# A two-layer graph network on one core: the second gather of the first layer becomes an accumulating one

## The chip, the cores and the metric

One core of a Trainium2 chip. The metric is device time in microseconds of one launch; lower is better. Before the change the median of 3 runs is 4833.23 us (4825.9 to 4849.17).

## The reference, cut to what matters

3125 nodes with 160 features (64 scalars and 32 vectors of three components), 100000 edges sorted by destination. Layer 0 is an attention layer over the edges, layer 1 a convolution with a segment sum. Of layer 0 the part that the change touches is the message of an edge, the sum of a row of its source node and a row of its destination node:

```python
s_n, v_n = _equiv_layernorm(s, v, gamma_s, beta_s, gamma_v)
src, dst = (edge_index[0], edge_index[1])
msg_s = (s_n @ Ws_src)[src] + (s_n @ Ws_dst)[dst]
msg_v = jnp.einsum('ncx,cd->ndx', v_n, Wv_src)[src] + jnp.einsum('ncx,cd->ndx', v_n, Wv_dst)[dst]
y0, y1 = (rsh[:, 0], rsh[:, 1:4])
w1 = rbf @ W_rbf
m1_s, m1_v = _cg_tp(msg_s, msg_v, y0, y1, w1[:, :CS], ...)
...
agg = jax.ops.segment_sum(alpha * h, dst, num_segments=n)
```

`_cg_tp` multiplies the message with the edge's weights and its direction; two more stages of small matrix products and such products follow, then a softmax over the edges of each destination and the segment sum.

## The kernel before

The kernel runs in stages, each of which all engines go through together.

- **Nodes.** 25 tiles of 128 nodes are normalised and multiplied with the weights. The rows for sources and destinations (160 floats, 640 bytes each) are written to two tables in HBM, `src_tab` and `dst_tab`.
- **Layer 0, first sweep.** The edges are worked off in 392 rounds of 256: 128 partitions, two edges on each (`G = 2`). This is the long stage, and the one that the change is in.
- **Layer 0, softmax and segment sum** (`stage_c`): maxima by scans, exponentials, then 49 windows whose sums GpSimd adds to `sum_tab` with accumulating transfers to HBM (line 698).
- **Layer 1.** Again 392 rounds, with one gathered table (`hid_tab`, line 721, two indirect transfers in a round), and 49 accumulating transfers to `agg_tab` (line 698). Then the output.

Each engine has its own program, written out by hand, and waits for the others at semaphores. `loop_steps` runs a function `stage(t)` for t = 0, 1, 2, ...; every part of it is called with an offset, so `gather0(t + 3)` works three rounds ahead of t. A step object `v` names the buffers of a round: `slot8` is round modulo 8, `par` modulo 2, `sslot` the half of the index buffer (four rounds share one load of indices; they are a group, whose first round has `place` 0).

In a round of the first sweep:

- **SP** (`sp0`) loads the indices of a group (`load_places`, line 487) when the group two before it has all its gathers landed (semaphores `LA["ga"]`), loads the inputs of the weights (`load_rbf`, line 496), and stores the result of the round two before (`store`, line 507, to `h_tab`).
- **GpSimd (POOL)** (`pool0`, `gather0`, line 658) issues four indirect transfers of 128 rows each: two from `src_tab` into `gat0`, two from `dst_tab` into `gatd`. Before them it waits until VectorE has used up the buffers (`LA["m"]`), and at the first round of a group for the indices (`LA["ix"]`). In the profile's rows `gat0` is called ACC and `gatd` SC, for the large tiles that hold them; each has 8 buffers. The transfers of a round raise `LA["ga"][slot8]` by 64.
- **VectorE (DVE)** (`stage0`) adds the two rows of the round (`messages`, line 1478, behind the wait for `LA["ga"]`), makes the products of round t+1 (`products0` and what follows, lines 1503 to 1529, the last of which raises `LA["m"]`), and between these works on round t-1 (lines 1540 to 1593) and t-2 (lines 1603 and 1612). Line 1503 waits for the sum of line 1478.
- **TensorE (PE)** transposes the products (line 800) and multiplies them with weights (lines 792, 822, 824, 847, 849); **ScalarE (ACT)** copies, weighs and applies the sigmoid.

The order in `stage0` before:

```python
gated(t + -1, total)
added = messages(t + 1, total)
ups = gated_up(t + -1, total)
done = summed(t + -1, total, ups)
parts = products0(t + 1, total, added)
scaled(t + -1, total, done)
```

## Time and profile before

| what | value |
|---|---|
| median of 3 runs | 4833.23 us |
| lowest, highest | 4825.9, 4849.17 us |
| span of the profiled execution, first to last instruction | 3828.1 us |
| what lies around the span, by the median | 1005.1 us |
| busy in the span: PE, PEld, DVE, ACT, POOL | 89%, 69%, 92%, 81%, 67% |
| first sweep of layer 0 in the span | about 86 to 2218 us |
| softmax and segment sum of layer 0, nodes between the layers | about 2218 to 2656 us |
| rounds of layer 1 | about 2656 to 3772 us |
| mean granted TensorE clock | 0.974 of full speed |

The profiled execution has no time of its own in the list beside its span; the 1005.1 us are the median less that span, and hold what runs before the first and after the last instruction of the program.

How to read it: the busy share of an engine is the share of the span in which it executed something that isn't a branch, a semaphore or the issue of a DMA. The idle time before a group of instructions is given with what ended it: "<-issue" is time in which the engine waited for nothing that the profile shows. An indirect transfer on POOL counts as busy while its descriptors are made, not while its bytes move; in what follows "a transfer on POOL" is that time. VectorE's instructions overlap a little in the rows, so a short wait between two of them may not show as idle time.

### The profile page before, as it was taken

How to read it: one execution, taken by the hardware profiler on the slowest of the kernel's cores; microseconds unless marked ns; L12 is line 12 of the kernel's file. 1: busy time of each engine (PE TensorE's matmuls, PEld its weight loads, DVE VectorE, ACT ScalarE, POOL GpSimd, SP SyncE). 2: the span in 40 equal slices, each digit the busy share in tenths (PEclk: the TensorE clock that was granted, in tenths of full speed). 3: DMA queues.
4: the chain of work that ended last, by engine and by line, in shares of the span. 5: the costliest groups of instructions: out<-in, count | busy, mean ns of one | idle time of the engine just before them, and what ended most of it. 6: DMA issues, size and time to landing. Idle time of an engine off the chain costs nothing. (4 is left out here: it accounts for less than half of the span.)

```text
span 3828.1 us, 96308 instructions
## 1 busy us (share of the span) xinstructions
PE 3407.1 (89%) x21340; PEld 2641.0 (69%) x21340; DVE 3541.0 (92%) x12738; ACT 3089.1 (81%) x11217; POOL 2570.9 (67%) x2469
## 2 busy tenths in 40 slices
PE   4899999999999999999999939976999999999997
PEld 3888888888888888888888838864333333333335
DVE  5999999999999999999999978874999999999995
ACT  4888899899989988988899847754787877778774
POOL 1777777777777777777777711111777777777772
PEclk8999999999999999999999979987999999999999
DMA  4333333333333333333333359971333433343333
GB/s 110 89 95 92 92 95 94 92 95 93 95 94 93 95 92 94 93 93 93 94 93 95 93 186 270 274 204 44 92 94 95 95 94 95 95 95 93 95 94 115
DMA packets 299642, 411.02 MB, mean 107 GB/s; under 512 B 98580, under 2 KB 234772, under 8 KB 299316
## 3 DMA queue, kind: packets, MB, share of 16 engines
q0 software_dynamic: 127008, 208.99, 24.2%
q1 hardware_dynamic: 172564, 201.26, 16.3%
q8 instruction: 24, 0.39, 0.0%
q14 instruction: 46, 0.38, 0.0%
HBM read 309.09 MB, written 100.94 MB: 107 GB/s over the span
## 5 line engine op out<-in xcount | busy, mean ns | idle before, releaser
L658 POOL DMA_INDIRECT SC<-dst_tab,idx x784 | 904.5, 1154 | 238.8 <-issue 237.3
L721 POOL DMA_INDIRECT ACC<-hid_tab,idx x784 | 811.4, 1035 | 348.6 <-issue 340.3
L658 POOL DMA_INDIRECT ACC<-src_tab,idx x784 | 758.5, 967 | 313.1 <-issue 164.2
L800 PE MATMUL TR<-ident,M 128*128 128x128 f32 x4704 | 664.4, 277 | 136.9 <-DVE M L1529 135.5
L800 PEld LDWEIGHTS TR<-ident,M 128*128 128x128 f32 x4704 | 520.1, 141 | 229.9 <-DVE M L1529 229.8
L1124 ACT ACTIVATE MT<-TR 128x768 f32<-128x768 f32 x784 | 596.9, 825 | 3.5 <-PE TR L800 3.5
L1113 ACT ACTIVATE ACC<-W,ACC 128x64 f32<-128x64 f32 x2352 | 577.7, 336 | 0.0
L849 PE MATMUL HP<-w_hv,MT 128*128 128x128 f32 x3136 | 520.2, 288 | 0.0
L824 PE MATMUL E<-w_mv,MT 128*128 128x128 f32 x3136 | 476.7, 275 | 0.0
L824 PEld LDWEIGHTS E<-w_mv,MT 128*128 128x128 f32 x3136 | 436.6, 191 | 0.0
L1306 ACT ACTIVATE ACC<-TR,y 128x128 f32<-128x128 f32 (+1 forms) x1568 | 417.2, 551 | 1.3 <-PE TR L982 1.2
L849 PEld LDWEIGHTS HP<-w_hv,MT 128*128 128x128 f32 x3136 | 413.2, 192 | 0.0
L1306 ACT ACTIVATE TAB<-TR,y 128x128 f32<-128x128 f32 (+1 forms) x1568 | 412.7, 422 | 0.0
L997 PE MATMUL HP<-M,ohE 128*128 128x480 f32 x800 | 374.4, 591 | 20.2 <-DVE M L1853 18.9
L792 PE MATMUL W<-w_rbf,rbf 128*128 128x224 f32 x1568 | 364.2, 355 | 15.9 <-DMA rbf<-in_rbf_line 13.7
L997 PE MATMUL E<-M,ohE 128*128 128x480 f32 x768 | 358.7, 590 | 17.5 <-DVE M L1853 16.1
L822 PE MATMUL E<-w_ms,MT 128*128 128x168 f32 x1568 | 355.0, 308 | 7.4 <-issue 4.7
L982 PEld LDWEIGHTS TR<-w_edge,ACC 64*128 64x128 f32 x1568 | 119.4, 186 | 322.5 <-ACT TAB L1306 157.5
L982 PE MATMUL TR<-w_edge,ACC 64*128 64x224 f32 x1568 | 255.9, 403 | 32.7 <-ACT TAB L1306 30.3
L1111 ACT ACTIVATE ACC<-W,ACC 128x96 f32<-128x96 f32 x784 | 272.4, 347 | 11.5 <-issue 11.5
L792 PEld LDWEIGHTS W<-w_rbf,rbf 128*128 128x128 f32 x1568 | 268.1, 192 | 16.8 <-issue 13.8
L847 PE MATMUL HP<-w_hs,MT 128*128 128x64 f32 x1568 | 265.7, 251 | 3.0 <-ACT MT L1124 3.0
(278 smaller groups left out, 7662.5 us busy)
## 6 DMA issues: line engine op xcount, KB each, us to landing
h_tab<-ACC SPq DMA_DIRECT2D x392, 160.0 KB
SC<-h_tab SPq DMA_DIRECT2D x50, 640.0 KB, 4.8
TAB<-h_tab SPq DMA_DIRECT2D x48, 640.0 KB, 5.2
ACC<-in_e64T SPq DMA_DIRECT2D x98, 256.0 KB
ACC<-src_tab,idx POOLq DMA_INDIRECT x784
SC<-dst_tab,idx POOLq DMA_INDIRECT x784
ACC<-hid_tab,idx POOLq DMA_INDIRECT x784, 3.4
agg_tab<-ACC POOLq DMA_DIRECT2D x49, 240.0 KB, 4.0
```

The costliest lines, as they stand in the source:

```text
L658: pool.indirect_dma_start(gat[:, v.slot8, g, :], None, table.ap(), bass.IndirectOffsetOnAxis(ap=idx[:, v.sslot, c + g:c + g + 1], axis=0))\
L721: pool.indirect_dma_start(gat1[:, v.slot8, g, :], None, hid_tab.ap(), bass.IndirectOffsetOnAxis(ap=idx[:, v.sslot, c:c + 1], axis=0))\
L792: ins = nc.tensor.matmul(W1[:, 224 * g:224 * (g + 1)], rbf[:, v.sslot, v.place, g, :], w_rbf[:, :], start=True, stop=True)
L800: ins = nc.tensor.transpose(to[:, b * G + g, :], Mt[:, g, lo:lo + w], ident[:, :])
L822: nc.tensor.matmul(E1[:, 0, ES * g:ES * (g + 1)], MT[:, 0, g, :], w_ms0[:, :], start=True, stop=True)
L824: ins = nc.tensor.matmul(E1[:, 1, P * g:P * (g + 1)], MT[:, 1 + b, g, :], w_mv0[:, b, :], start=(b == 0), stop=(b == 1))
L849: ins = nc.tensor.matmul(HP[:, P + P * g:P + P * (g + 1)], MT2[:, 1 + b, g, :], w_hv0[:, b, :], start=(b == 0), stop=(b == 1))
L982: ins = nc.tensor.matmul(Wr[v.par][:, g, 0:224], hid[hg, v.qslot, P * v.quad_place:P * (v.quad_place + 1)], w_edge1[hg, :], start=True, st ...
L997: ins = nc.tensor.matmul(AG[v.sslot][:, 0:MW], ohE[:, v.slot, g, :], M[:, v.par, g, :], start=(v.place == 0 and g == 0), stop=(v.place == ...
L1113: ins = nc.scalar.activation(o[:, 160 + 64 * k:224 + 64 * k], w[:, 160:224], ACT.Copy, scale=y_at(v, g, 1 + k))
L1124: nc.scalar.activation(dst[:, 0:3].rearrange("p k g e -> p (k g e)"), tr[:, 0:3 * G, :].rearrange("p a e -> p (a e)"), ACT.Copy).then_inc( ...
L1306: ins = nc.scalar.activation(WS[v.slot][:, g, P * k:P * k + hi - lo], wg_[:, lo:hi], ACT.Copy, scale=y1[:, v.sslot, c:c + 1])
```

## The change

The rows of the destination are no longer fetched into a buffer of their own and added by VectorE. They are fetched by an indirect transfer that adds them to the rows of the source, which are already in `gat0`. Such a transfer may only be issued when the plain gather below it has landed, so the gather of the source rows is asked for six rounds ahead instead of three, and the adding transfer three rounds ahead. SP's load of the indices moves from seven rounds ahead to eight. `gatd` and `messages` are gone; the wait for the landed rows stands at the head of `products0`.

```diff
-        gatd = scf[:, 0:8 * G * D].rearrange("p (b g f) -> p b g f", b=8, g=G)
...
             def sp0(t, total):
-                load_places(t + 7, total)
+                load_places(t + 8, total)
                 load_rbf(t + 5, total)
                 store(t + -2, total)
-            loop_steps(sp, Q, NS, False, 7, 2, sp0)
+            loop_steps(sp, Q, NS, False, 8, 2, sp0)
...
+            def gather_src(v, total):
+                if not inside(v, total):
+                    return
+                if v.past(7):
+
+                    wait(LA["m"], v.num - 6)
                 if v.place == 0:
                     wait(LA["ix"][v.sslot], v.sup_round(16))
...
+                for g in range(G):
+                    c = 2 * v.place + g
+                    pool.indirect_dma_start(gat0[:, v.slot8, g, :], None, src_tab.ap(),
+                                            bass.IndirectOffsetOnAxis(ap=idx[:, v.sslot, c:c + 1], axis=0))\
+                        .then_inc(LA["ga"][v.slot8], 16)
+
+            def add_dst(v, total):
+
+                if not inside(v, total):
+                    return
+                wait(LA["ga"][v.slot8], v.slot_round(64, 8) - 32)
+                for g in range(G):
+                    c = 2 * Q + 2 * v.place + g
+                    pool.indirect_dma_start(gat0[:, v.slot8, g, :], None, dst_tab.ap(),
+                                            bass.IndirectOffsetOnAxis(ap=idx[:, v.sslot, c:c + 1], axis=0),
+                                            compute_op=ALU.add)\
+                        .then_inc(LA["ga"][v.slot8], 16)
 
             def pool0(t, total):
-                gather0(t + 3, total)
-            loop_steps(pool, Q, NS, False, 3, 0, pool0)
+                gather_src(t + 6, total)
+                add_dst(t + 3, total)
+            loop_steps(pool, Q, NS, False, 6, 0, pool0)
...
-            def messages(v, total):
-
-                if not inside(v, total):
-                    return
-                dve.wait_ge(LA["ga"][v.slot8], v.slot_round(64, 8))
-                row = gat0[:, v.slot8, :, :]
-                return ch.count(TT(row, row, gatd[:, v.slot8, :, :], ALU.add))
...
+            def products0(v, total):
+
+                if not inside(v, total):
+                    return None
                 dve.wait_ge(LA["ga"][v.slot8], v.slot_round(64, 8))
...
-                added = messages(t + 1, total)
                 ups = gated_up(t + -1, total)
                 done = summed(t + -1, total, ups)
-                parts = products0(t + 1, total, added)
+                parts = products0(t + 1, total)
```

The queue of POOL in the middle of the first sweep, with what each row waits for (a_m is `LA["m"]`, a_ix0 the landing of a group's indices). Before, two rounds read:

```order
L658 DMA ACC<-src_tab,idx 128x160 [waits a_m]
L658 DMA ACC<-src_tab,idx 128x160
L658 DMA SC<-dst_tab,idx 128x160 x2
L644 REGISTER_ALU
L644 REGISTER_ALU [waits a_m]
L658 DMA ACC<-src_tab,idx 128x160 [waits a_ix0]
L658 DMA ACC<-src_tab,idx 128x160
L658 DMA SC<-dst_tab,idx 128x160 x2
```

and now (a_ga4 and a_ga5 are the landings in two of the eight buffers):

```order
L657 DMA ACC<-src_tab,idx 128x160 [waits a_m]
L657 DMA ACC<-src_tab,idx 128x160
L668 DMA ACC<-dst_tab,idx 128x160 [waits a_ga4]
L668 DMA ACC<-dst_tab,idx 128x160
L643 REGISTER_ALU
L643 ISA [waits a_m]
L657 DMA ACC<-src_tab,idx 128x160 [waits a_ix0]
L657 DMA ACC<-src_tab,idx 128x160
L668 DMA ACC<-dst_tab,idx 128x160 [waits a_ga5]
L668 DMA ACC<-dst_tab,idx 128x160
```

There are four transfers in a round as before; the last two now write the same tile as the first two, of an earlier round, and wait for its landing.

At the very start of the stage POOL's queue now reads:

```order
L657 DMA ACC<-src_tab,idx 128x160 [waits s_tab0d,a_ix0]
L657 DMA ACC<-src_tab,idx 128x160 x7
L668 DMA ACC<-dst_tab,idx 128x160 [waits a_ga0]
L668 DMA ACC<-dst_tab,idx 128x160
L657 DMA ACC<-src_tab,idx 128x160 [waits a_ix1]
```

Eight plain gathers stand ahead of the first adding pair, where two stood ahead of the first pair from `dst_tab`.

## Rows read from the trace of the kernel before

**Rows 1.** Busy time by stage: first sweep, rounds of layer 1.

```profile
core 0: us, PE busy (x) PEld busy (x) DVE busy (x) ACT busy (x) POOL busy (x), PEclk, DMA share, GB/s
102.00:2218.00 2116.00, 1979.12 (x15485) 1855.71 (x15484) 2096.20 (x8519) 1906.76 (x6968) 1643.54 (x1551) 1.00 0.35 93
2656.00:3772.00 1116.00, 1037.45 (x3332) 422.85 (x3332) 1039.24 (x3527) 869.41 (x3284) 860.43 (x833) 0.99 0.39 93
```

**Rows 2.** Groups on POOL, 102 to 2218 us: busy, mean ns, idle before.

```profile
L658 POOL DMA_INDIRECT SC<-dst_tab,idx x775 | 894.3, 1154 | 236.1 <-issue 234.6 <-DVE M L1529 1.5
L658 POOL DMA_INDIRECT ACC<-src_tab,idx x776 | 750.7, 967 | 236.7 <-issue 162.1 <-DVE M L1529 74.6
```

**Rows 3.** Timeline of the start of the sweep, POOL's gathers and VectorE's addition.

```profile
84.02 0.95 POOL L658 DMA_INDIRECT SC<-dst_tab,idx  x1 [0.30 <-issue]
85.27 0.94 POOL L658 DMA_INDIRECT ACC<-src_tab,idx  x1 [0.30 <-issue]
...
86.55 0.49 DVE L1478 TENSOR_TENSOR ACC<-ACC,SC 128x320 f32<-128x320 f32 x1 [17.83 <-DMA SC<-dst_tab,idx]
...
91.57 0.49 DVE L1478 TENSOR_TENSOR ACC<-ACC,SC 128x320 f32<-128x320 f32 x1 [2.47 <-DMA SC<-dst_tab,idx]
...
96.54 0.49 DVE L1478 TENSOR_TENSOR ACC<-ACC,SC 128x320 f32<-128x320 f32 x1 [1.88 <-DMA SC<-dst_tab,idx]
```

**Rows 4.** Timeline in mid-sweep: POOL's transfers and VectorE beside them.

```profile
1006.25 0.95 POOL L658 DMA_INDIRECT SC<-dst_tab,idx  x1 [0.30 <-issue]
...
1007.50 1.55 POOL L658 DMA_INDIRECT SC<-dst_tab,idx  x1 [0.30 <-issue]
...
1010.68 0.49 DVE L1478 TENSOR_TENSOR ACC<-ACC,SC 128x320 f32<-128x320 f32 x1
...
1011.09 0.35 DVE L1546 TENSOR_TENSOR svy<-E,ACC 128x192 f32<-128x192 f32 x1
...
1023.42 1.81 POOL L658 DMA_INDIRECT SC<-dst_tab,idx  x1 [0.30 <-issue]
```

**Rows 5.** VectorE's addition, 102 to 2218 us: group, and its waits.

```profile
L1478 DVE TENSOR_TENSOR ACC<-ACC,SC 128x320 f32<-128x320 f32 x388 | 190.4, 491 | 20.3 <-DMA SC<-dst_tab,idx 18.3
```

**Rows 6.** Groups on POOL in layer 1, 2656 to 3772 us.

```profile
L721 POOL DMA_INDIRECT ACC<-hid_tab,idx x784 | 811.4, 1035 | 348.6 <-issue 340.3 <-DVE M L1853 7.7 <-ACT ACC L1317 0.6
L698 POOL DMA_DIRECT2D agg_tab<-ACC x49 | 50.1, 1022 | 9.5 <-issue 9.4
```

**Rows 7.** First transfer of layer 1: the idle time before it.

```profile
2656.38 1.09 POOL L721 DMA_INDIRECT ACC<-hid_tab,idx  x1 [102.84 <-issue]
```

**Rows 8.** The accumulating transfers' line 698: ns min/median/max.

```profile
L698 POOL DMA_DIRECT2D sum_tab<-ACC x49: 841/848/986, 2303.6 to 2552.7; - x49
L698 POOL DMA_DIRECT2D agg_tab<-ACC x49: 984/1023/1055, 2699.9 to 3771.9; - x49
```

**Rows 9.** DMA issues: KB each, median us from issue to landing.

```profile
ACC<-hid_tab,idx POOLq DMA_INDIRECT x784, 3.4
agg_tab<-ACC POOLq DMA_DIRECT2D x49, 240.0 KB, 4.0
...
sum_tab<-ACC POOLq DMA_DIRECT2D x49, 82.0 KB, 5.2
...
gam_v<-in_gamma_v SPq DMA_DIRECT2D x3, 0.1 KB, 1.9
```

**Rows 10.** SP's timeline around a load of indices.

```profile
1021.19 0.35 SPq L487 DMA_DIRECT2D idx<-in_idx_line  x1
1021.79 0.34 SPq L507 DMA_DIRECT2D h_tab<-ACC  x1
```

More of the change, by code:

```diff
@@ L646, in _ @@
             pool.wait_ge(s_tab0d, 160)
-            def gather0(v, total):
+            def gather_src(v, total):
                 if not inside(v, total):
                     return
-                if v.past(4):
-                    wait(LA["m"], v.num - 3)
+                if v.past(7):
+                    wait(LA["m"], v.num - 6)
                 if v.place == 0:
                     wait(LA["ix"][v.sslot], v.sup_round(16))
-                for c, gat, table in ((2 * v.place, gat0, src_tab), (2 * Q + 2 * v.place, gatd, dst_tab)):
-                    for g in range(G):
-                        pool.indirect_dma_start(gat[:, v.slot8, g, :], None, table.ap(),
-                                                bass.IndirectOffsetOnAxis(ap=idx[:, v.sslot, c + g:c + g + 1], axis=0))\
-                            .then_inc(LA["ga"][v.slot8], 16)
+                for g in range(G):
[13 more added lines that the diff above has]
+                        .then_inc(LA["ga"][v.slot8], 16)
             def pool0(t, total):
-                gather0(t + 3, total)
-            loop_steps(pool, Q, NS, False, 3, 0, pool0)
+                gather_src(t + 6, total)
+                add_dst(t + 3, total)
+            loop_steps(pool, Q, NS, False, 6, 0, pool0)
             pool.wait_ge(s_flag, 1)
@@ L1470, in y_of @@
                 return ax(y_all[:, bass.ds(v.column(0), 1), k:k + 1], (4, G), *dims)
-            def messages(v, total):
-                if not inside(v, total):
-                    return
-                dve.wait_ge(LA["ga"][v.slot8], v.slot_round(64, 8))
-                row = gat0[:, v.slot8, :, :]
-                return ch.count(TT(row, row, gatd[:, v.slot8, :, :], ALU.add))
-            def products0(v, total, added):
+            def products0(v, total):
                 if not inside(v, total):
                     return None
-                ch.wait(added)
+                dve.wait_ge(LA["ga"][v.slot8], v.slot_round(64, 8))
                 dve.wait_ge(LA["ws"], v.num + 1)
```

## The prediction

> **What bounds the kernel now.** I read the stages first, then the groups of one engine in the stage that changes, then its timeline, and last the rows of other transfers that price the new one.
>
> By stages, VectorE looks like the bound of the first sweep: it is busy 2096.20 of 2116.00 us, POOL only 1643.54 [rows 1]. That is the share that misleads here. The groups on POOL show an idle time of 0.30 us before every one of its 1551 transfers, never much more, and nearly all of it "issue": it is what POOL needs between two transfers. Busy and idle time together are 894.3 + 750.7 + 236.1 + 236.7 = 2117.8 us [rows 2], the whole of the 2116 us. So **POOL is occupied without a break**, exactly like VectorE. 1551 transfers are 387.75 rounds, one in 5.46 us.
>
> Which of the two leads? At the start of the sweep VectorE waits 2.47 and 1.88 us for the gathered rows, and its additions start 5.02 and 4.97 us apart [rows 3]: POOL's pace with undisturbed transfers, 4 x (0.95 + 0.30) = 5.00 us. POOL never gets a lead. In mid-sweep single transfers are stretched from 0.95 to 1.55 and 1.81 us with the same 0.30 us before them, which no transfer is while VectorE waits [rows 3, 4]. The mean stretch brings the round from 5.00 to 5.46 us. A gather that ends at 1007.50 + 1.55 = 1009.05 is followed by its addition at 1010.68, 1.63 us later; at the start it was 86.55 - (84.02 + 0.95) = 1.58 us, with VectorE idle and waiting [rows 3]. The addition thus begins about when the rows land. The profile books only 18.3 us of waiting there over 388 rounds [rows 5], but with overlapping records short waits don't show. VectorE's own work is 2096.20 / 387.75 = 5.41 us a round, POOL's 5.46 us: two bounds side by side, POOL's the tighter by a hair.
>
> Layer 1 confirms the reading of POOL: 811.4 + 348.6 + 50.1 + 9.5 us, less the 102.84 us before the first transfer, are 1116.8 us in a stretch of 1116 [rows 6, 7]. There too it never rests, and a transfer takes 1.035 us on the mean, 0.09 above the undisturbed one.
>
> **The change, part by part.** The time of reference is the profiled execution's span, 3828.1 us, and the 1005.1 us around it, which is the median 4833.23 by construction; nothing around the span changes.
>
> *VectorE's addition goes.* From its start to the next instruction are 1011.09 - 1010.68 = 0.41 us [rows 4]; VectorE's work falls from 5.41 to 5.00 us a round. Were VectorE the only bound, that would be 0.41 x 392 = 161 us. It is covered by POOL, which still issues four transfers a round and needs 5.46 us for them, so I count it as 0. The wait for the rows moves behind lines 1546, 1554 and 1557, and only line 1503 and what follows now queue behind it; harmless, because the round is set elsewhere.
>
> *Two of four gathers become adding ones.* POOL's time for the plain ones is 2 x (0.967 + 0.305) = 2.54 us, for the pair from `dst_tab` 2 x (1.154 + 0.305) = 2.92 us, 5.46 together [rows 2]. No row shows an indirect transfer that adds. The nearest are the direct accumulating ones of line 698: 0.85 us into `sum_tab` against 0.95 for a plain gather, and in layer 1 1.02 against 1.035 [rows 6, 8]. By them the price is between -0.10 and 0 us more than a gather. From above: an adding row is read, read again at its destination and written, three runs where a copy has two; half as much again is 0.95 x 0.5 = +0.48 us. I take +0.10 us, near the rows of line 698 but on the dear side, because they need no indices and this one needs both. Two a round: 0.20 x 392 = **+78 us** (bounds -78 and +376).
>
> *The stretches.* I keep them as they are, 0.46 us a round. If all went, the round would be 5.00 us, -180 us; if they grew by as much, +180 us. They come with VectorE's instructions, of which one goes, but the rest will run closer together.
>
> The Trainium skill (SBUF — State Buffer, "Who interferes with whom") says that a VectorE instruction with two inputs in SBUF contends with a GpSimd instruction that reads SBUF. The removed addition is one of 16 such instructions in a round and some tenth of their time, so by that page a tenth of the stretches would go with it, 0.05 us a round, 18 us in all, and the sum below would be 4920 us. Rows 3 and 4 agree that only a working VectorE stretches the transfers; which of its instructions does, they don't say.
>
> *The new wait of POOL for the landing of the source rows.* Between that gather and its adding transfer stand 12 others, some 16 us, and rows land 1.6 us after the gather's end [rows 4]. Cost 0. If landing took over 16 us it would stop the queue.
>
> *The loads of indices.* POOL now asks for a group's indices at the gather six rounds ahead, while SP may overwrite that half only when the adding transfers of the group two before have landed. In POOL's queue between the last of those and the first gather that needs the new indices stands one round: 5.46 + 0.30 us. In it must pass the landing of the adding transfer, SP's reaction, and the small load. Before, three more rounds stood there. An accumulating transfer lands 4.0 us after its issue in layer 1 and 5.2 in the segment sum [rows 9], that is 3.0 to 4.4 us after POOL's end of it; the load lands about 1.9 us after its issue (a small load) [rows 9], and I allow 0.3 us for SP. So 5.2 to 6.6 us against 5.8: between 0 and 0.8 us lost in four rounds. I take 0.2, which is 0.05 x 392 = **+20 us** (bounds 0 and +80). Behind SP's wait now stand its stores, one round later than before; 0.6 us after the load they follow [rows 10], and `hst` has four buffers, so no one waits. That cover ends at two rounds of delay.
>
> *Start and end.* The first products need 8 gathers and 2 adding transfers instead of 4 gathers: 6 x 1.25 = 7.5 us later. At the end the last three rounds have only adding transfers and run at VectorE's 5.0 us; about even. **+7 us.**
>
> The transfers themselves: all DMA engines are busy 0.35 of the sweep [rows 1]. The adding ones move more, but even twice the present share stays below the whole. Cost 0. `gatd` leaves SC free, with no effect on others.
>
> **Sum:** 4833 + 78 + 20 + 7 = **4938 us**, a round of about 5.7 us. A measurement of this kernel can tell about 0.5% (24 us) from no change.
>
> **The rivals.**
>
> *Faster: VectorE was the bound.* If POOL's stretches are only what lets it keep step with VectorE (both need 5.4 us, and a transfer never runs into the next round), a shorter VectorE round shortens them, and if adding costs like copying the round falls to 5.0 to 5.1 us: 4833 - 161 + 7 = 4679 us, or 4720 with half of the stretch left. For it: the 2096.20 us of busy time, 99%, and that POOL's and VectorE's periods agree so well. Against it: layer 1's POOL, stretched as well with a busy VectorE, and the additions that start as rows land. Chance 0.18.
>
> The Trainium skill (Perfetto Trace Analysis, "Identifying the Most-Contended Engine") says to optimise first the engine of highest occupancy, which by the busy shares is VectorE; that rule stands behind this rival. The rows on POOL, busy and issue time together, speak against its reading here.
>
> *No change.* Adding costs what copying costs, indices arrive in time, stretches stay: 4833 + 7 = 4840 us. For it: line 698. Chance 0.20.
>
> *Much slower: indices or landings set the round.* The adding transfer lands as late as in the segment sum or later. Then POOL's queue runs dry once in four rounds, 0.8 us or more: 4833 + 78 + 80 + 7 = 4998 us; with an adding transfer at +0.25 us, 5115 us. It decides from a landing of 3.6 us after POOL's end. For it: rows 9. Against it: the segment sum's landing was taken with the DMA engines nearly full. Chance 0.20.
>
> The change does what it says: the order of POOL's queue shows it.
>
> **How the numbers follow.** Forecast 0.42 (4938 us; its own range 4880 to 5040), the rivals 0.18, 0.20 and 0.20. The range must take in most of the slow rival and half of the fast one: 4720 to 5130 us. Faster by over 0.5%, below 4809 us: 0.18 and a little of "no change" by fewer stretches, 0.24. Within 0.5%: 0.16. Slower: 0.60.
>
> **What would show it.** In the new profile of the sweep: VectorE's busy time near 5.0 of 5.7 us a round, with waits at line 1503 for the DMA; POOL's busy and issue time still the whole sweep; line 668 near 1.25 us, line 657 near 0.97; at one in four rounds a gap before line 657 of 0 to 0.8 us. The prediction is wrong if line 668's mean is at or below 1.05 us and the round below 5.4, or if POOL shows gaps that wait for VectorE's line 1529.

## The result, and the profile after

The changed kernel takes **4493.55 us** (median of 4 runs, 4476.52 to 4500.86), the kernel before beside it 4841.2 us (4 runs, 4825.9 to 4868.19): a ratio of **0.9274, 95% interval 0.924 to 0.9308**. Forecast was 4938 us in 4720 to 5130: the change is 7% faster, outside the range and on the other side.

One thing has to be said before any line is read: **the execution whose rows stand ahead of the prediction was not one of those that were timed**, nor like them. It spans 3828.1 us. In the runs below each profiled execution has a time of its own. The kernel before, profiled again, took 4862.71 us and spans 4861.1: 1.6 us lie around the span, not 1005. The same goes for the changed kernel, 4500.86 us and a span of 4499.2. The experiments ran on six chips; on five the kernel before took 4783 to 4846 us, on the sixth 3818.76 us (median of 11), like the first profile. All executions on one chip are of one kind, so this text speaks of the chips; whether it is the chip itself or something that went with it, no run tells. Nearly all that follows is about what those five do and the first profile does not. e1 to e4 shared a chip, so did e5 to e8, e9 to e11, e12 to e14 and e15 to e17, and e18 ran on the sixth; between chips ratios are compared, not times.

By stages, the changed kernel (first sweep, rounds of layer 1), columns as in [rows 1]:

```profile
95.00:2661.00 2566.00, 2081.12 (x15576) 1932.78 (x15576) 1976.51 (x8188) 1948.60 (x7014) 2086.58 (x1557) 0.97 0.40 77
3100.00:4420.00 1320.00, 1110.12 (x3284) 448.66 (x3284) 1028.53 (x3464) 868.53 (x3240) 864.34 (x819) 0.91 0.33 78
```

and the kernel before, profiled again (e1_before), the same stages:

```profile
95.00:3010.00 2915.00, 2249.62 (x15527) 2111.54 (x15526) 2099.47 (x8547) 1946.70 (x6992) 1722.97 (x1557) 0.89 0.25 68
3459.00:4790.00 1331.00, 1114.25 (x3298) 448.82 (x3298) 1036.48 (x3492) 868.11 (x3252) 871.86 (x822) 0.91 0.32 77
```

The sweep is 349 us shorter, layer 1 the same: the gain lies where the edit is. A round (four transfers of GpSimd) takes 2566 / (1557 / 4) = 6.59 us now, 2915 / (1557 / 4) = 7.49 us in e1_before, and took 5.46 us in the first profile. In e1_before no engine is busy for more than 77% of the sweep, and VectorE is idle for 28% of it, where in [rows 1] VectorE never rested and GpSimd was occupied throughout. TensorE's clock is granted at 0.89 of full on the mean; between its two levels, 1.2 and 2.4 GHz, that is the lower one for 22% of the time. In the changed kernel the mean is 0.97.

GpSimd's groups in the sweep (name, busy us, mean ns, idle time before and what ended it), the changed kernel:

```profile
L668 POOL DMA_INDIRECT ACC<-dst_tab,idx x782 | 1305.5, 1669 | 238.3 <-issue 238.3
L657 POOL DMA_INDIRECT ACC<-src_tab,idx x775 | 781.1, 1008 | 236.1 <-issue 215.0 <-DVE M L1533 21.0
```

e1_before:

```profile
L658 POOL DMA_INDIRECT ACC<-src_tab,idx x778 | 976.4, 1255 | 939.1 <-DVE M L1529 699.9 <-issue 239.1
L658 POOL DMA_INDIRECT SC<-dst_tab,idx x779 | 747.4, 959 | 237.7 <-issue 236.8 <-DVE M L1529 0.9
```

In the changed kernel these four numbers fill the sweep: 1305.5 + 781.1 + 238.3 + 236.1 = 2561 of 2566 us. **GpSimd is occupied without a break**, as [rows 2] had it. In e1_before it waits 699.9 us for VectorE's last product. So nothing is gained by less work: the adding transfer costs 1.669 us where the plain one beside it costs 1.008. GpSimd works more and the kernel is faster.

Who was late? VectorE's line 1603 (1607 now) uses TensorE's last product of a round. Its group in the middle of the sweep, in the first profile (500 to 2100 us) and in e1_before (500 to 2500):

```profile
L1603 DVE TENSOR_TENSOR tG<-HP,ACC 128x192 f32<-128x192 f32 x293 | 103.0, 352 | 0.0
```

```profile
L1603 DVE TENSOR_TENSOR tG<-HP,ACC 128x192 f32<-128x192 f32 x268 | 95.4, 356 | 528.9 <-remote 365.7 <-PE HP L849 155.1 <-issue 8.1
```

No idle time before it in the first profile, against 528.9 us in 268 rounds of e1_before, most of it "remote": a signal that the profile ties to no instruction's end. The same group in the changed kernel (500 to 2500):

```profile
L1607 DVE TENSOR_TENSOR tG<-HP,ACC 128x192 f32<-128x192 f32 x304 | 107.8, 355 | 188.1 <-PE HP L861 101.2 <-remote 84.9
```

It still waits, in 195 of 304 rounds, but for 2.1 us at the longest; in e1_before the longest of these waits is 6.2 us. The timeline of e1_before shows one such case (start, length, engine, line, idle time before it):

```profile
1020.34 0.66 PE L849 MATMUL HP<-w_hv,MT 128*128 128x128 f32 x4
...
1022.30 0.82 PE L800 MATMUL TR<-ident,M 128*128 128x128 f32 x6
...
1025.70 0.36 DVE L1603 TENSOR_TENSOR tG<-HP,ACC 128x192 f32<-128x192 f32 x1 [4.33 <-remote]
...
1027.38 0.35 DVE L1529 TENSOR_TENSOR M<-ACC 128x192 f32<-128x192 f32 x1
...
1027.79 1.54 PE L800 MATMUL TR<-ident,M 128*128 128x128 f32 x6 [4.66 <-DVE M L1529]
...
1028.68 0.94 POOL L658 DMA_INDIRECT ACC<-src_tab,idx  x1 [4.25 <-DVE M L1529]
```

The product that line 1603 waits for ends at 1021.00, by the profile; line 1603 starts 4.70 us later. VectorE stands, its products (line 1529) come late, TensorE stands for 4.66 us and then runs its transposes in 1.54 us instead of 0.82, at half the clock, and GpSimd stands for 4.25 us. Call this **a late signal of TensorE**. (These traces lack some of the semaphores' records, so "remote" by itself proves little; the 4.70 us between the product's end and the start of line 1603 don't depend on it. The end of a matmul is modelled by the profiler, so the product itself may have been late.)

### The profile page after: what moved, and what is told of

Its sections match the earlier page's. It is cut to its first block and busy times, and to the rows that moved or that the text cites. A ratio compares the mean times of both kernels' runs of the same rounds, so it can differ in the third digit from the quotient of the medians.

```text
span 4499.2 us, 96352 instructions
## 1 busy us (share of the span) xinstructions
PE 3588.3 (80%) x21340; PEld 2740.0 (61%) x21340; DVE 3413.8 (76%) x12346; ACT 3129.9 (70%) x11217; POOL 3025.2 (67%) x2469
## 2 busy tenths in 40 slices
DMA packets 374905, 411.01 MB, mean 91 GB/s; under 512 B 98580, under 2 KB 322580, under 8 KB 374580
## 5 line engine op out<-in xcount | busy, mean ns | idle before, releaser
L668 POOL DMA_INDIRECT ACC<-dst_tab,idx x784 | 1308.6, 1669 | 238.9 <-issue 238.9
L733 POOL DMA_INDIRECT ACC<-hid_tab,idx x784 | 830.4, 1059 | 554.7 <-issue 352.8
L657 POOL DMA_INDIRECT ACC<-src_tab,idx x784 | 790.0, 1008 | 312.7 <-issue 217.5
L861 PE MATMUL HP<-w_hv,MT 128*128 128x128 f32 x3136 | 536.5, 295 | 0.0
L1009 PE MATMUL HP<-M,ohE 128*128 128x480 f32 x800 | 408.0, 636 | 43.2 <-DVE M L1856 29.9
L1009 PE MATMUL E<-M,ohE 128*128 128x480 f32 x768 | 396.0, 642 | 48.0 <-issue 24.4
L1507 DVE TENSOR_TENSOR M<-ACC 128x192 f32<-128x192 f32 x392 | 140.2, 358 | 376.2 <-DMA ACC<-dst_tab,idx 369.2
L1174 ACT ACTIVATE ACC<-HP 128x128 f32<-128x128 f32 x392 | 109.1, 278 | 447.1 <-DVE ACC L1616 383.9
L804 PE MATMUL W<-w_rbf,rbf 128*128 128x224 f32 x1568 | 388.4, 373 | 15.7 <-DMA rbf<-in_rbf_line 13.6
L1164 ACT ACTIVATE M<-V,ACC 128x96 f32<-128x96 f32 x784 | 252.2, 373 | 115.3 <-DVE V L1571 66.8
```

Source lines behind the costliest of these rows:

```text
L657: pool.indirect_dma_start(gat0[:, v.slot8, g, :], None, src_tab.ap(), bass.IndirectOffsetOnAxis(ap=idx[:, v.sslot, c:c + 1], axis=0))\
L668: pool.indirect_dma_start(gat0[:, v.slot8, g, :], None, dst_tab.ap(), bass.IndirectOffsetOnAxis(ap=idx[:, v.sslot, c:c + 1], axis=0), comp ...
L733: pool.indirect_dma_start(gat1[:, v.slot8, g, :], None, hid_tab.ap(), bass.IndirectOffsetOnAxis(ap=idx[:, v.sslot, c:c + 1], axis=0))\
L804: ins = nc.tensor.matmul(W1[:, 224 * g:224 * (g + 1)], rbf[:, v.sslot, v.place, g, :], w_rbf[:, :], start=True, stop=True)
L861: ins = nc.tensor.matmul(HP[:, P + P * g:P + P * (g + 1)], MT2[:, 1 + b, g, :], w_hv0[:, b, :], start=(b == 0), stop=(b == 1))
L1009: ins = nc.tensor.matmul(AG[v.sslot][:, 0:MW], ohE[:, v.slot, g, :], M[:, v.par, g, :], start=(v.place == 0 and g == 0), stop=(v.place == ...
```

## The experiments

Rounds and clock in the table are read from one view of each kernel, busy time between 500 and 2500 us: 2000 us by a fourth (with a memset a fifth) of GpSimd's instructions, and the mean granted clock. The ratio is to the kernel before on the same chip, with its interval.

| run | edit | round, us | clock | median, us | ratio |
|---|---|---|---|---|---|
| e1_before | none | 7.46 | 0.89 | 4854.16 | 1.001 (0.9988 to 1.0032) |
| e2_no_add | VectorE's addition left out | 7.77 | 0.91 | 4948.13 | 1.0166 (1.0091 to 1.0241) |
| e3_plain | the change, transfers not adding | 7.82 | 0.90 | 4975.75 | 1.0247 (1.0198 to 1.0296) |
| e4_after | the change | 6.56 | 0.98 | 4502.07 | 0.9292 (0.9254 to 0.933) |
| e5_plain_pad | e3 + memset of 1280 | 6.79 | 0.97 | 4587.23 | 0.9589 (0.956 to 0.9619) |
| e6_before_pad | before + memset of 1280 | 6.83 | 0.96 | 4567.19 | 0.9536 (0.9501 to 0.957) |
| e7_plain_pad_half | e3 + memset of 640 | 7.32 | 0.94 | 4778.72 | 0.9975 (0.9946 to 1.0003) |
| e8_after_pad1 | change + memset of 192 in layer 1 | 6.43 | 1.00 | 4453.26 | 0.932 (0.9291 to 0.9349) |
| e9_before_pe | before + 6 transposes | 7.64 | 0.92 | 4907.62 | 1.0162 (1.0106 to 1.0218) |
| e10_after_pe | change + 6 transposes | 6.55 | 0.99 | 4501.45 | 0.9322 (0.9274 to 0.937) |
| e11_after_pad | change + memset of 640 | 7.47 | 1.00 | 4846.53 | 1.0042 (0.9995 to 1.009) |
| e12_before_dve | before + VectorE's 960 | 6.86 | 0.98 | 4613.37 | 0.9534 (0.9496 to 0.9572) |
| e13_before_pe12 | before + 12 transposes | 7.73 | 0.94 | 5010.67 | 1.0342 (1.0299 to 1.0384) |
| e14_half | half of the change | 7.04 | 0.89 | 4702.56 | 0.9731 (0.969 to 0.9772) |
| e15_half_u16 | e14, 16 rounds in a pass | 7.08 | 0.91 | 4726.47 | 0.9759 (0.9715 to 0.9803) |
| e16_before_u16 | before, 16 rounds in a pass | 7.39 | 0.89 | 4853.08 | 1.0025 (1.0 to 1.0049) |
| e17_after_u16 | change, 16 rounds in a pass | 6.62 | 0.96 | 4511.57 | 0.9311 (0.9272 to 0.9349) |
| e18_half_dve | e14 + VectorE's 760, sixth chip | 7.23 | 0.97 | 4511.51 | 1.1792 (1.1763 to 1.1821) |

### One part of the change alone

e1_before is the kernel before as it stands, e4_after the changed one.

> The kernel before, unchanged, profiled once more. The profile of before spans 3828 us, its runs take about 4840 us, and in the profile after span and time differ by 1.6 us only. Theory A (the first profiled execution of before was an undisturbed one, the timed ones are not): the new profile spans about 4830 us, layer 1 takes about 1340 us as after the change, and the round of the first sweep about 7.3 us instead of 5.46. Rival B (some 1000 us always lie around the span of this kernel, and the change took them away): the new profile spans 3828 us again and its round is 5.46 us.

> The change itself beside the three others on the same chip: about 0.927 of before, 4490 us, with a round of 6.5 us in the first sweep and a layer 1 of 1340 us. If this chip or this execution is undisturbed, its span would be shorter, and the unchanged layer 1 would tell: 1116 us.

e2_no_add takes VectorE's addition out. The wait for the landed rows moves to `products0`, as in the change; all else stays.

```diff
-                row = gat0[:, v.slot8, :, :]
-                return ch.count(TT(row, row, gatd[:, v.slot8, :, :], ALU.add))
+                return 0
```

> The kernel before with VectorE's addition left out and nothing in its place: the rows of the destination are still fetched into their own buffer and not used, so the messages lack them. Theory A (VectorE's work or its waits behind the addition set the disturbed round): about 4500 us or less, as fast as the change. Rival (the addition is covered and the gain of the change comes from the lead of the gathers or from the kind of transfer): within 1% of before, 4800 to 4850 us.

e3_plain is the change with plain transfers.

```diff
-                                            bass.IndirectOffsetOnAxis(ap=idx[:, v.sslot, c:c + 1], axis=0),
-                                            compute_op=ALU.add)\
+                                            bass.IndirectOffsetOnAxis(ap=idx[:, v.sslot, c:c + 1], axis=0))\
```

> The change with the second pair of transfers as plain gathers (it overwrites the source rows, so the messages lack them). It tells what adding costs in a transfer: the adding one took 1.67 us on POOL in the profile after, 0.6 more than a plain one. Theory (POOL sets the round of 6.56 us after the change): the round falls by up to 2 x 0.6 = 1.2 us, 4490 - 400 = 4050 to 4150 us. Rival (other waits set it, such as landings or the loop): within 1% of the change, 4450 to 4500 us.

Measured: both are **slower** than before, by 1.7 and 2.5%, and both intervals lie above 1. VectorE's freed 0.41 us bring nothing, and neither do the new order and the longer lead. The whole gain hangs on the transfers being adding ones, and these cost GpSimd more. That leaves two readings: adding transfers help by what they are, or by being slow.

### GpSimd slowed by work that does nothing

In each round GpSimd clears unused SBUF before its gathers: 1280 floats (e5 on e3's code, e6 on the kernel before) or 640 (e7).

```diff
+            def pad(v, total):
...
+                nc.gpsimd.memset(tabf[:, 2600:3880], 0.0).then_inc(LA["pad"], 1)
...
             def pool0(t, total):
+                pad(t + 3, total)
                 gather0(t + 3, total)
```

> The changed kernel with plain gathers in place of the adding ones (so the rows of the source are overwritten, not summed, as in e3_plain, whose round was 7.85 us), and in each round one GpSimd memset of 1280 floats per partition into unused SBUF, some 1.25 us by the 0.75 us of the memset of 768. GpSimd's round is then 4 x (1.0 + 0.3) + 1.25 = 6.45 us, that of the changed kernel (6.56). Theory (pace): it is the pace of GpSimd that lets TensorE keep its clock, not what the transfers do. Then work that does nothing makes the kernel faster: a round of 6.5 to 6.7 us, 4470 to 4550 us, half of full clock in under 8% of the sweep. Rival 1 (the adding transfer itself, its traffic or its landing, is what helps): the memset adds nothing good; the round stays at 7.85 us or grows by up to 1.25: 4976 to 5450 us. Rival 2 (GpSimd is late in some rounds only): about 5100 us.

> The kernel before, all of its work in place (VectorE's addition too), with the same memset in each round. Pace theory: the round falls from 7.48 to 6.5 to 6.8 us, 4840 - 392 x 0.8 = 4530 us (4470 to 4600), and VectorE's addition is worth nothing. If VectorE's addition mattered beside the pace, e6 would be slower than e5 by up to 0.41 x 392 = 161 us. Rival 1: 4840 us or more, up to 5330.

> As e5_plain_pad, with a memset of half the size, 640 floats, some 0.64 us: GpSimd's round would be 5.85 to 5.9 us. What it tells is how near to the engines' own work (VectorE 5.0 us) the pace may go. If the pace theory holds down to there: 4976 - 392 x 1.9 = 4230 us. If the alternation of TensorE's clock comes back between 5.9 and 6.5 us: 4500 to 4900 us. Rival 1: 4976 to 5200 us.

GpSimd in the middle of the sweep, e6_before_pad:

```profile
L658 POOL DMA_INDIRECT SC<-dst_tab,idx x586 | 687.1, 1172 | 178.7 <-issue 176.5 <-DVE M L1538 2.1
L658 POOL DMA_INDIRECT ACC<-src_tab,idx x585 | 619.2, 1059 | 169.9 <-issue 94.5 <-POOL TAB L667 39.6 <-DVE M L1538 35.8
L667 POOL MEMSET TAB<- 128x1280 f32 x293 | 347.0, 1184 | 0.1
```

e7_plain_pad_half:

```profile
L657 POOL DMA_INDIRECT ACC<-src_tab,idx x547 | 603.4, 1103 | 517.8 <-DVE M L1541 379.8 <-issue 136.6 <-POOL TAB L677 1.5
```

The kernel before, with every part of its work and 1.18 us of nothing in each round, is 4.6% faster (e6). e5 against e3 is 0.9589 / 1.0247, 6.4% by the same edit. It is **the pace**, not the adding. With half the memset GpSimd would need 5.9 us a round; it waits 379.8 us for VectorE again, and only a part of the gain is left (e7). e5 and e6 do not quite reach the changed kernel's 0.93. In e6 half of the difference is GpSimd's own time: its gathers are stretched to 1172 and 1059 ns, and with the issue time it needs (687.1 + 619.2 + 347.0 + 176.5 + 94.5 + 39.6) / 293 = 6.70 us a round, against 6.56 in e4; the other 0.13 us are waits for VectorE. In e5 GpSimd needs 6.4 us and waits for VectorE for 0.39 us a round.

### The same in layer 1

```diff
+                nc.gpsimd.memset(flat[:, 8000:8192], 0.0).then_inc(LB["pad"], 1)
```

> The changed kernel, with a memset of 192 floats (0.24 us) before each round's gathers in layer 1, whose round is now 3.38 us where its GpSimd needs about 2.9 us. If the pace theory holds there too, with a round of 3.15 us: 4502 - 0.25 x 392 = 4405 us. If layer 1's round is kept up by something else, the memset either hides (4502 us) or adds (up to 4502 + 94 = 4596 us).

Ratio 0.932 against 0.9292 of e4: nothing. From its first to its last gather layer 1 takes 1337 us in e8 and 1336 in e4, so the memset falls into GpSimd's waits. Layer 1's round is not helped by so small a pace; a larger one was not tried.

### More work for TensorE

Before it waits for VectorE's products, TensorE transposes the identity six times (twelve in e13) into places that it overwrites next.

```diff
-                pe.wait_ge(LA["m"], v.num + 1)
                 if v.past(1):
                     pe.wait_ge(LA["c1"], v.num)
+                for k in range(6):
+                    nc.tensor.transpose(TR1[:, k % 6, :], ident[:, :], ident[:, :])
+                pe.wait_ge(LA["m"], v.num + 1)
```

> The kernel before, GpSimd's queue untouched; TensorE makes six more transposes of the constant identity in each round, into the PSUM places that it overwrites right after, before it waits for VectorE's products: 0.82 us at the full clock. TensorE's work is then some 5.7 us a round (4.9 + 0.8), which is above VectorE's 5.4. Theory (the clock is what costs the round its 2 us, and it falls after TensorE has stood idle): the idle stretches are filled, half of full clock falls from 22% to under 8% of the sweep, and the round is 5.8 to 6.6 us in spite of more work: 4190 to 4500 us. Rival (the pace of GpSimd itself matters, by the transfers' spacing; the clock is a symptom): the round stays near 7.5 us or grows by part of the 0.8: 4840 to 5150 us. Rival 2 (more TensorE work makes the clock fall more often): 4950 us and more.

> The same six transposes in the changed kernel, whose TensorE has 1.2 us of idle time in a round of 6.56 us set by GpSimd. Theory: 0.8 us fit in, half of full clock falls from 5% to 0 to 3% of the sweep; the round is GpSimd's as before: 4470 to 4510 us, ratio to the changed kernel 0.99 to 1.0. If TensorE's time mattered beside GpSimd's pace: up to 4700 us.

In e9 the clock rises from 0.89 to 0.92 and the round does not fall: 7.64 us. So **half clock is not what costs the round its 2 us**, as my theory had it, and an upper bound agrees (an estimate from e1_before): at half clock for 22% of a round of 7.46 us, TensorE loses at most 0.11 x 7.46 = 0.8 us, even if it set the pace all the time. The late signals are still there in e9 (line 1605's "remote" waits, 436.6 us). In e10 the six transposes fit in and cost nothing, as expected.

### The changed kernel slowed further

```diff
+                nc.gpsimd.memset(tabf[:, 2600:3240], 0.0).then_inc(LA["pad"], 1)
```

> The changed kernel with a memset of 640 floats (0.65 us, as in e7_plain_pad_half) in each round of GpSimd. If GpSimd's occupied time is what sets the round of the changed kernel, all of it shows: 6.56 + 0.65 = 7.2 us, 4502 + 255 = 4757 us (4730 to 4770), and the alternation is not less than before (half clock 5% or less). If the changed kernel were helped further by a slower pace, under 4700 us; if something else set its round, 4500 to 4600 us.

GpSimd and VectorE's two lines with TensorE's product, e11_after_pad:

```profile
L668 POOL DMA_INDIRECT ACC<-dst_tab,idx x535 | 998.2, 1866 | 163.1 <-issue 163.1
L657 POOL DMA_INDIRECT ACC<-src_tab,idx x535 | 541.6, 1012 | 125.1 <-issue 81.3 <-POOL TAB L678 43.8
L678 POOL MEMSET TAB<- 128x640 f32 x268 | 327.0, 1220 | 0.0
...
L1616 DVE TENSOR_TENSOR tG<-HP,ACC 128x192 f32<-128x192 f32 x267 | 92.7, 347 | 0.0
```

GpSimd sets the round of the changed kernel: what is added to it shows in full, and more (7.47 us; 7.2 expected), and the records are longer too, the memset's 1.22 us against 0.65 in e7 and the adding transfer's 1.87. They overlap, though (busy and idle time add up to 2155 of 2000 us), so how much of the round each takes they don't tell. There is not one late signal left and the clock is full all through, although TensorE is busy only 1434.96 of 2000 us. An idle TensorE as such brings neither; it idles here in every round, but for 1.3 us at the longest.

### Who may keep the pace, and half of the change

e12 gives VectorE one more instruction, e13 TensorE twelve transposes; e14 makes only one of the two destination gathers an adding one, and VectorE adds the other (160 floats).

```diff
+                    ch.count(TT(tabf[:, 2600:3560], tabf[:, 2600:3560], tabf[:, 2600:3560], ALU.max))
                 gated(t + -1, total)
```

```diff
+                    to, how = (gat0, dict(compute_op=ALU.add)) if g == 0 else (gatd, {})
+                    pool.indirect_dma_start(to[:, v.slot8, g, :], None, dst_tab.ap(),
```

> The kernel before with one more VectorE instruction at the head of each round (the larger of 960 unused floats and themselves, some 1.15 us by the 0.49 us of the addition of 320). VectorE's work is then 5.4 + 1.15 = 6.55 us a round. Theory A (any engine that keeps a pace of some 6.5 us calms the round): 6.5 to 6.8 us a round, 4450 to 4580 us, although the engine that bounds the kernel got more to do. Theory B (it must be GpSimd that paces, because its transfers, asked for in a rush after each stall, start the next one, or because VectorE that never rests is part of the trouble): the stalls of 4 us stay on top of a round of 6.55, 7.5 to 8.7 us, 4840 to 5300 us.

> As e9_before_pe with twelve transposes, so that TensorE's own work is 4.9 + 1.64 = 6.5 us a round: TensorE keeps the pace. In e9 (six) half of full clock fell from 22% to 15% of the sweep and the round was 7.64 us. Theory A: 6.6 to 7.0 us, 4500 to 4650 us. Theory B, or a TensorE whose late signals are the stall itself: 7.6 to 8.5 us, 4900 to 5250 us.

> Half of the change: of a round's two destination gathers one adds to the source rows, the other goes to a buffer and VectorE adds it (160 floats, 0.28 us). GpSimd's own time is 1.97 + 1.27 + 2 x 1.31 = 5.87 us a round. Pace theory, by e7_plain_pad_half (5.87 us too, and measured at a ratio of 0.9975 with rounds of 7.2 us): ratio 0.97 to 1.0, irregular rounds of 7.0 to 7.4 us. If the adding transfers help by themselves, each by half of what two bring: ratio 0.965 and GpSimd never waiting. If the round were GpSimd's time: 5.9 us, 4240 us, ratio 0.88.

e12 is the plainest result of the study: **VectorE, the busiest engine by [rows 1], gets 1.15 us more to do in each round, and the kernel before is 4.7% faster.** Theory A (any engine may keep the pace) holds for VectorE and GpSimd. For TensorE it stays untested: e13 is 3.4% slower, but its transposes made no floor under the round. 99 of its 391 rounds follow the one before within 6 us, against one in e12, so TensorE did not hold the pace of 6.5 us that it was to keep. That its added work only stands behind its own late signals fits, and is not shown. e14 falls between, and its GpSimd still waits for VectorE, as the pace theory said. Pace is not all: with the same 5.87 us of work for GpSimd, e7 has a ratio of 0.9975 and e14 one of 0.9731.

In e12 the rounds run at 6.4 us, and a late signal stands out. Two rounds of e12_before_dve, a normal one and the next:

```profile
1192.67 0.61 PE L824 MATMUL E<-w_mv,MT 128*128 128x128 f32 x4
...
1194.09 1.15 DVE L1617 TENSOR_TENSOR TAB<-TAB 128x960 f32<-128x960 f32 x1
...
1195.16 0.29 DVE L1540 SCALAR_TENSOR_TENSOR la<-E,adot 128x144 f32<-128x144 f32 x1
...
1199.24 0.61 PE L824 MATMUL E<-w_mv,MT 128*128 128x128 f32 x4
...
1200.51 1.15 DVE L1617 TENSOR_TENSOR TAB<-TAB 128x960 f32<-128x960 f32 x1
...
1205.04 0.31 DVE L1540 SCALAR_TENSOR_TENSOR la<-E,adot 128x144 f32<-128x144 f32 x1 [3.38 <-remote]
```

The product of line 824 ends at 1193.28 and at 1199.85; line 1540, which uses it, starts at once after line 1617 in the first, and 3.38 us late in the second, 5.2 us after the product's end.

### Where the late signals come from

I counted rounds of over 8.3 us by the distance of VectorE's line 1516 (1503 in the kernels before, 1517 in e15) from one round to the next. In e12 there are 29, and all stand at the second to fourth of the 8 rounds of a loop's pass; in e14 99 of 391, 72 of them at the second and third. (The 33 and 117 in the expectation of e18 were miscounted.) That pointed to the turn of the loop. So the first sweep was written out with 16 rounds in a pass.

```diff
+            r = 4 if sups == NS else 2
...
-            with eng.Fori(2, end, 2) as base:
-                for u in range(2 * q):
+            with eng.Fori(r, end, r) as base:
+                for u in range(r * q):
```

> e14_half with 16 rounds written out in each pass of the loop of the first sweep instead of 8, on every engine; nothing else changes. In e14_half the rounds run at 5.15 us and nearly all long ones (10.2 and 10.3 us on the mean, with TensorE's signals late by 5 to 8 us) are the second and third of the 8 of a pass. Theory C (the late signals come with the pass of a loop, when engines go back to its start): the long rounds come half as often, at two of 16 places; the mean round falls from 7.08 to 6.1 to 6.3 us, ratio to the kernel before 0.89 to 0.91, some 4330 us. Rival (they come by time or by data, and only happen to be in step with 8 rounds): the mean round stays at 7.0 to 7.2 us, ratio 0.97. Rival 2 (they come with the amount of code, which is doubled): more of them, ratio over 1.

> The kernel before with 16 rounds in a pass instead of 8. There long rounds are found at all places. Theory C with echo (a late signal starts a disorder that has no slack to die out in, and that starts further ones): fewer starts, a round of 7.0 us or less, ratio 0.93 to 0.97. If in this kernel stalls breed stalls without an outside start: ratio 0.99 to 1.01.

> The changed kernel with 16 rounds in a pass. GpSimd is occupied without a break and sets 6.55 us; its transfers are a little stretched after each disorder (adding transfer 1.57 us median, 1.67 mean). Theory: nearly the same, a round of 6.45 to 6.55 us, ratio 0.92 to 0.93; if the disorder after a pass cost more than is seen, down to 0.91.

Theory C falls: e15 has 91 long rounds, not half of 99, 65 of them in two heaps at the first to fourth and the eleventh to thirteenth of 16, and a ratio of 0.9759 against 0.9731. The kernel before (e16, 1.0025) and the changed one (e17, 0.9311) don't gain by the longer pass either. With half as many turns of the loop the disorder comes as often. It keeps its own distance (2769 us / 99 = 28 us in e14, 30 in e15) and a place in the loop can hold it in step, but does not make it. Nor is it the loading of code: in the DMA view of e1_before the queues of instructions have 24 and 46 packets in the whole span, and none between 500 and 2500 us.

### A try for a version that beats both

> e14_half (one adding gather in a round instead of two; GpSimd 5.87 us, VectorE 5.15 us a round) with one more VectorE instruction at the head of each round, the larger of 760 unused floats and themselves, some 0.95 us: VectorE keeps a pace of 6.1 us. It is the try for a version that beats the kernel before and the changed one: if the calm holds down to 6.1 us, rounds of 6.1 to 6.4 us and 4330 to 4430 us, ratio 0.895 to 0.915. If the late signals come back between 6.4 (e12: calm but for 33 long rounds) and 5.15 (e14: 117 of 391), as in e7_plain_pad_half at 5.87 us: rounds of 6.7 to 7.2 us, 4550 to 4750 us, ratio 0.94 to 0.98.

This run fell on the sixth chip, where the kernel before takes 3818.76 us, and the try is 18% slower. The views of e18_half_dve there: layer 1, GpSimd's groups and VectorE's line 1616 in the sweep, and GpSimd beside the added instruction:

```profile
3362.00:4456.00 1094.00, 1031.60 (x3314) 421.30 (x3314) 1035.96 (x3519) 865.81 (x3275) 848.23 (x824) 1.00 0.40 94
```

```profile
L658 POOL DMA_INDIRECT ACC<-src_tab,idx x772 | 1196.8, 1550 | 235.3 <-issue 235.3
L670 POOL DMA_INDIRECT ACC<-dst_tab,idx x389 | 649.2, 1669 | 118.5 <-issue 118.5
L670 POOL DMA_INDIRECT SC<-dst_tab,idx x389 | 481.0, 1236 | 118.5 <-issue 118.5
...
L1616 DVE TENSOR_TENSOR tG<-HP,ACC 128x192 f32<-128x192 f32 x276 | 96.6, 350 | 0.0
```

```profile
1004.22 2.17 POOL L670 DMA_INDIRECT SC<-dst_tab,idx  x1 [0.30 <-issue]
1004.61 0.94 DVE L1630 TENSOR_TENSOR TAB<-TAB 128x760 f32<-128x760 f32 x1
1006.70 0.95 POOL L658 DMA_INDIRECT ACC<-src_tab,idx  x1 [0.30 <-issue]
```

No late signal; layer 1 runs at full clock, and from its first to its last gather it takes 1104 us, 1107 in the first profile and 1346 in e1_before. GpSimd is occupied without a break, 1196.8 + 649.2 + 481.0 + 235.3 + 118.5 + 118.5 = 2799 us for 386 to 389 rounds, 7.2 us each, and that is the round. Here every us for GpSimd costs a us, which is what the prediction said of the first profile. The adding transfer costs the same 1.669 us as on the other chips. What e18 was to tell, whether 6.1 us are calm on the five, it does not tell.

The changed kernel itself did not run on this chip. Estimate: its GpSimd needs 2 x (1.669 + 1.008) + 4 x 0.305 = 6.57 us a round, from the groups of the changed kernel above, against 5.46 us [rows 2], so 3819 + 1.11 x 392 = 4254 us, **some 11% slower** than before there. What speaks for it is that e18, with GpSimd the bound, behaves so; it was not measured.

## Why the prediction was wrong

- **"The 1005.1 us around it ... nothing around the span changes."** This is the step that failed. The 1005 us are not around the span: they are longer rounds inside it, 7.46 us instead of 5.46 in the sweep (784 us over 392) and 1331 us instead of 1116 in layer 1 (215 us), together 999 us. A difference of 26% between span and median was booked by construction, where it should have said that the profile is of another kind of execution.
- **"POOL is occupied without a break."** True of the first profile and of e18. False of the executions that were timed, where GpSimd waits 699.9 us for VectorE, until the change makes it true (2561 of 2566 us).
- **VectorE's addition, 0 us.** No gain, right; e2 without it is 1.7% slower than before.
- **An adding transfer at +0.10 us (bounds -0.10 and +0.48).** Mis-sized: 1.669 us against 1.008 for the plain one, +0.66, and +0.52 against the 1.154 us of the transfer that it replaces [rows 2]; both lie over the upper bound. The direct accumulating transfers of line 698 [rows 8] were the wrong neighbour. Where GpSimd is the bound that is 2 x 0.52 x 392 = 408 us at the least, not 78.
- **The stretches, kept.** The plain gathers next to adding ones are hardly stretched, 1.008 us; the adding ones may be: what one takes undisturbed in mid-sweep was not isolated. This term is small beside the others.
- **The new wait for the landing, 0 us.** Right: all 238.3 us before line 668 are issue time. **The loads of indices, +20 us.** Nothing: no wait for them shows in the sweep's groups.
- **The rivals.** "Faster: VectorE was the bound" had the sign and not the mechanism: e12 gives VectorE more work and gains. That slowing an engine could make the pipeline faster was in none of my cases. Its 4720 us "with half of the stretch left" is also a slip: half of 0.46 us on top of 5.00 is a round of 5.23 us, 4833 - 90 + 7 = 4750 us.
- **The signs I named.** Line 668 near 1.25 us (1.669), line 657 near 0.97 (1.008), GpSimd occupied throughout (yes), VectorE waiting for the DMA at its first product (yes, line 1507, 261.6 us between 500 and 2500), the round near 5.7 us (6.59). So the pricing of GpSimd's queue was sound in kind; on these chips the kernel before was not bound by it. That the new time lies below the old one and not above it comes from the first step.

The Trainium skill (Perfetto Trace Analysis, "Identifying the Most-Contended Engine") says to optimise the engine of highest occupancy first. In e1_before no engine is above 77% (TensorE, 2249.62 of 2915 us; its weight loads 72%) and VectorE has 72%; e2, which relieves VectorE, is slower, and e12, which loads it, is faster. Where all engines rest for a fifth of the time, as here, occupancy named no bound.

**What the change does, then**, on the five chips: TensorE's signals come several us late now and then; the longest wait for one is 6.2 us in e1_before and 9.0 in e14. An unpaced pipeline of rounds of 5.0 to 5.5 us that follow at once meets such a signal about every third round (97 "remote" waits of line 1603 in 268 rounds, 3.8 us on the mean), and runs part of the next round at half clock. Where one engine holds the rounds at 6.4 us and more they come seldom (e12), stay short (the changed kernel, 2.1 us at the most) or don't show at all (e11). The adding transfers hold GpSimd, and so all others, at 6.56 us. That the slower pace makes the late signals rarer or shorter, and the kernel faster, is shown (e5, e6, e12); why TensorE's signals are late, on these chips and not on the sixth, and why only a fast round brings it on, stays open. The turn of the loop, the loading of code and VectorE's addition are not the cause, and half clock is too small to be it.

## What to carry to other kernels

Before a sum is made on a profile, set the profiled execution's own time against its span; if the median is far from the span, the profile shows another kind of execution, and a cost worked out on it holds for that kind alone. Where no engine is busy for more than four fifths of a stage and the rounds scatter, try a pad on one engine: a few lines tell whether an irregular pipeline loses more than the slowest engine does. And a gain that comes from pace can turn with the chip: measure such a change on more than one.

## What the runs showed of the hardware

- An indirect transfer that adds into SBUF occupies GpSimd for 1.67 us, a plain one of the same 128 rows for 0.95 to 1.01 us when nothing stretches it. The page of the profile counts 374905 DMA packets for the changed kernel and 299642 for the kernel before: (374905 - 299642) / 784 = 96 more in each adding transfer, at the same 411 MB.
- A long VectorE instruction stretches transfers strongly: beside the 0.94 us of e18's added instruction one takes 2.17 us, the next one 0.95. Of the transfers of e18 between 500 and 2500 us that overlap that instruction fully, the median is 2.17 (`dst_tab`) and 2.36 us (`src_tab`), of those that don't touch it 0.98 and 0.95. The Trainium skill (SBUF — State Buffer, "Who interferes with whom") says that a VectorE instruction with two inputs in SBUF contends with a GpSimd instruction that reads SBUF; the trace agrees, though the loss, some 1.2 us, is more than the instruction's own length; three shorter VectorE instructions, of 0.29 to 0.34 us, overlap the same transfer, and what each costs was not separated.
- Two kinds of executions of one program, by chip: 3819 and 4783 to 4846 us for the kernel before. The slower kind shows in both layers, with "remote" waits behind TensorE and a mean clock of 0.89 to 0.90; the faster has none of these waits and 0.97.
- TensorE at a busy share of 0.72 kept the full clock through the whole middle of the sweep in e11, and at 0.78 it was granted 0.89 in e1_before. Between 500 and 2500 us of e1_before it had stood idle for 1.9 to 7.2 us shortly before each of its 87 falls; in e11, where the longest idle time is 1.3 us, it never fell. Long idle times are not needed, though: in e18 the clock fell 30 times in the same stretch (mean 0.97), and no idle time of TensorE there is longer than 1.4 us.
